# Split queries and keys stored once and repeated by the reads, on one core of Trainium2

## The reference, cut to what matters

```python
h = _layernorm(x, ln_w, ln_b)             # then a causal convolution over three tokens, giving h
q, k, v = jnp.split(h @ attn_w, 3, axis=-1)
q = q * cos + _rotate_half(q) * sin       # 16 heads of 8 dimensions
k = k * cos + _rotate_half(k) * sin
scores = jnp.einsum('bqhd,bkhd->bhqk', q, k) / jnp.sqrt(jnp.float32(D))
scores = jnp.where(causal, scores, jnp.float32(-1e+30))
p = jax.nn.softmax(scores, axis=-1)
y = jnp.einsum('bhqk,bkhd->bqhd', p, v).reshape(B, T, C)
```

## Time and profile before

| | us |
|---|---|
| median of 3 runs | 341.47 (338.66 to 347.56) |
| the profiled execution, its own time | 340.81 |
| its span in the trace | 338.6 |
| PE busy | 315.3 (93% of the span) |
| DVE busy | 245.2 (72%) |
| ACT busy | 220.0 (65%) |
| POOL busy | 128.1 (38%) |
| all 16 DMA engines, mean rate over the span | 66 GB/s |

### The profile page before, as it was taken

One profiled execution on the slowest core, in us unless ns is written; L12 is line 12 of the kernel. 1 busy time (PEld: TensorE's weight loads), 2 busy tenths in 40 slices (PEclk: granted clock), 3 DMA queues, 4 the chain that ended last, 5 costly groups with the idle time before them and its releaser, 6 DMA issues.

```text
span 338.6 us, 6802 instructions
## 1 busy us (share of the span) xinstructions
PE 315.3 (93%) x2270; PEld 220.6 (65%) x2270; DVE 245.2 (72%) x758; ACT 220.0 (65%) x649; POOL 128.1 (38%) x183
## 2 busy tenths in 40 slices
PE   8799989998989999999989998998999999999886
PEld 3348778665554433345446998985778687878675
DVE  4988875784898988888811552479788877887576
ACT  1488885375365756756676765754676667686995
POOL 3455564110641444410640440410685434535400
PEclk9999999999999999999998999999999999999999
DMA  7590000076763430091001003100100000000002
GB/s 213 196 274 10 2 0 2 8 243 170 209 206 89 113 102 3 1 326 52 5 31 56 2 31 111 33 1 2 54 20 15 0 2 1 3 0 0 2 0 65
DMA packets 21881, 22.47 MB, mean 66 GB/s; under 512 B 3894, under 2 KB 18646, under 8 KB 21846
## 3 DMA queue, kind: packets, MB, share of 16 engines
q1 hardware_dynamic: 18982, 16.78, 17.4%
q10 hardware_dynamic: 2352, 4.20, 3.7%
q0 software_dynamic: 512, 1.05, 1.0%
HBM read 14.22 MB, written 7.60 MB: 64 GB/s over the span
## 4 chain that ended last, share of the span: by engine, by line
PE 58%; DVE 16%; ACT 14%; issue 5%; POOL 4%; DMA 3%; SPq 0%; ACTq 0%; POOLq 0%
PE PS L1388 51%; PE PS L1442 5%; DVE PS L872 5%; ACT big L1167 5%; ACT big L1364 3%; POOL big L529 2%; DVE big L690 2%; DVE big L715 2%; DMA big<-in_A_WkT 2%; ACT big L1305 1%; ACT big L1141 1%; DMA XN<-scr_y,pos 1%; DVE XN L667 1%; ACT cw L1141 1%; PE PS L1704 1%
## 5 line engine op out<-in xcount | busy, mean ns | idle before, releaser
L1388 PE MATMUL PS<-big 128*128 128x128 f32 (+10 forms) x592 | 93.3, 308 | 7.0 <-DVE big L690 2.1
L1388 PEld LDWEIGHTS PS<-big 128*128 128x128 f32 (+3 forms) x592 | 56.2, 150 | 39.7 <-DVE mB L872 18.2
L529 POOL TENSOR_TENSOR big<-big,urec 128x1024 f32<-128x1024 f32 x24 | 45.6, 1900 | 60.2 <-DVE urec L722 45.4
L1167 ACT ACTIVATE big<-big 128x154 f32<-128x154 f32 x192 | 60.5, 319 | 10.6 <-DVE big L690 5.6
L872 DVE CUSTOM_DVE_ANT_0 PS<-PS,later 128x128 f32<-128x128 f32 (+3 forms) x128 | 60.1, 517 | 8.9 <-PE PS L1388 7.7
L1305 ACT ACTIVATE big<-PS 128x1024 f32<-128x1024 f32 (+3 forms) x64 | 43.2, 701 | 25.0 <-PE PS L1388 25.0
L1141 ACT ACTIVATE big<-PS 128x1280 f32<-128x1280 f32 (+2 forms) x30 | 32.3, 1088 | 27.0 <-PE PS L1442 24.5
L1388 PE MATMUL PS<-kkC,XT 128*128 128x462 f32 (+1 forms) x96 | 36.0, 511 | 1.9 <-DVE big L715 1.9
L1167 ACT ACTIVATION_READ_ACCUMULATOR big<-big 128x1 f32 x192 | 36.2, 189 | 0.0
L517 POOL TENSOR_TENSOR rstd<-ve,minus_half 128x4 f32<-128x4 f32 (+2 forms) x13 | 13.2, 1017 | 56.3 <-DVE ve L662 56.3
L1388 PEld LDWEIGHTS PS<-vwCm,big 128*128 128x128 f32 x256 | 30.8, 192 | 3.9 <-ACT big L1141 1.3
(11 more groups left out here) (192 smaller groups left out, 499.7 us busy)
## 6 DMA issues: line engine op xcount, KB each, us to landing
scr_qk<-big SPq DMA_DIRECT2D x12, 384.0 KB, 3.3
big<-scr_qk SPq DMA_DIRECT2D x16, 288.0 KB
big<-in_wv ACTq DMA_DIRECT2D x1, 2048.0 KB, 7.9
scr_x<-zrow SPq DMA_DIRECT2D x2, 448.0 KB, 6.9
scr_y<-big SPq DMA_DIRECT2D x2, 448.0 KB, 3.4
X<-in_x ACTq DMA_DIRECT2D x2, 256.0 KB, 3.3
big<-in_A_WoT ACTq DMA_DIRECT2D x1, 512.0 KB, 4.7
cw<-in_C_Wk SPq DMA_DIRECT2D x1, 512.0 KB, 5.2
```

The costliest lines, as they stand in the source:

```text
L529: pool.tensor_tensor(pn[:, 0:GH * P].rearrange("p (h k) -> p h k", h=GH), Pt[u % 3][:, :, 0:KM], r.to_broadcast([P, GH, KM]), ALU.mult).th ...
L1167: i = act.activation(Pt[u % 3][:, h, :], Pt[u % 3][:, h, :], ACT.Exp, accum_out=usum[:, u % 3, h:h + 1])
L1388: return pe.matmul(o, lhsT, rhs, start=start, stop=stop)
```

## The change

What it does, in six points:

1. `scr_qk` holds each part once (24 rows for keys, 24 for queries, per sequence). The six writes of a sequence are 128x512 of bf16 (128 KB) each instead of 384 KB.
2. The reads repeat rows. The keys of a group are still one DMA into 72 partitions, but its source has three outer steps of stride 0, then the 24 rows. The queries of a group are three DMAs, one for each x, into 24 partitions each; the source of each has three outer steps of stride 0, then 8 rows. `stack_ready` is awaited at 64 instead of 32.
3. On VectorE the second norm b is moved ahead of the split of sequence 0; `weigh_router` is moved from step 1 of the attention to before `rotate(1)`.
4. Folds: the second `queries_keys` stands at fold 25 instead of 30, the turn of norm b at 17 instead of 26, and the tasks m begin after fold 25 instead of 31. 24 folds lie between the tasks instead of 18; four tasks (`M_TWICE`) are followed by two folds.
5. For sequence 0 the constant columns of `vaug` are set by two memsets on POOL instead of two copies on ScalarE.
6. TensorE's wait ahead of the first task is for the copies of all but the last two folds; the whole of them is awaited at task 2. The first turn of maxima stands after fold 40.

```diff
         PS = ctx.enter_context(nc.psum_tensor("PS", [P, 8, 512], F32))
-        scr_qk = nc.dram_tensor("scr_qk", (B, 2, SPLIT, HB, T), BF16, kind="Internal").ap()
+        scr_qk = nc.dram_tensor("scr_qk", (B, 2, 3, SPLIT // 9, HB, T), BF16, kind="Internal").ap()
...
         F_UNIT = (3, 6, 9)
-        F_QKV = (14,30)
-        F_LN = 26
-        F_LATE = 32
-        F_VALUES = 42
-        F_MAX = 45
+        F_QKV = (14, 25)
+        F_LN = 17
+        F_LATE = 26
+        F_VALUES = 38
+        F_MAX = 41
+        M_TWICE = (5, 9, 13, 17)
...
             for b in range(B):
                 for a in range(3):
                     sp.wait_ge(part_ready[b], a + 1)
-                    sp.dma_start(scr_qk[b, 1].rearrange("(x y d) h t -> y (d h) x t", x=3, y=3)[a],
-                                 P3[:, 1, a, :].unsqueeze(1).to_broadcast([P, 3, T])).then_inc(scr_written[b], 16)
-                    sp.dma_start(scr_qk[b, 0].rearrange("(x y d) h t -> x (d h) y t", x=3, y=3)[a],
-                                 P3[:, 0, a, :].unsqueeze(1).to_broadcast([P, 3, T])).then_inc(scr_written[b], 16)
+                    for j in (1, 0):
+                        sp.dma_start(scr_qk[b, j, a].rearrange("d h t -> (d h) t"), P3[:, j, a, :]).then_inc(scr_written[b], 16)
                 if b:
                     store_maxima(0)
                 sp.wait_ge(scr_written[b], 16 * 6)
                 for g in range(HB // HG):
                     hs = slice(HG * g, HG * g + HG)
-                    sp.dma_start(ks[b][0:SPLIT, hs, :], scr_qk[b, 1, :, hs, :]).then_inc(stack_ready[b][g], 16)
-                    sp.dma_start(qs[b][0:SPLIT, hs, :], scr_qk[b, 0, :, hs, :]).then_inc(stack_ready[b][g], 16)
+                    parts = [scr_qk[b, j, :, :, hs, :].rearrange("a d h t -> a d (h t)") for j in range(2)]
+                    sp.dma_start(ks[b][0:SPLIT, hs, :].rearrange("r h t -> r (h t)"),
+                                 parts[1].unsqueeze(0).to_broadcast([3, 3, SPLIT // 9, HG * T])).then_inc(stack_ready[b][g], 16)
+                    for x in range(3):
+                        sp.dma_start(qs[b][SPLIT // 3 * x:SPLIT // 3 * (x + 1), hs, :].rearrange("r h t -> r (h t)"),
+                                     parts[0][x].unsqueeze(0).to_broadcast([3, SPLIT // 9, HG * T])).then_inc(stack_ready[b][g], 16)
...
             pool.wait_ge(part_ready[1], 3)
+            pool.wait_ge(preC_act, sum(j[2] for j in PREC[:F_VALUES]))
+            v = vaug[:, 0].rearrange("p t h m -> p (t h) m")
+            pool.memset(v[:, :, HDB:HDB + 1], 1.0).then_inc(v_ready, 1)
+            pool.memset(v[:, :, HDB + 1:32], 0.0).then_inc(v_ready, 1)
             split_maxima(1)
...
@@ -860,11 +875,12 @@
             add_tile("A", NT - 1)
             ln_u_stats(1)
             rotate(0)
+            ln_b_stats(1)
             add_rotated()
+            ln_apply("b", U, XN, 1)
             split_first()
-            ln_b_stats(1)
-            ln_apply("b", U, XN, 1)
             convolve(1)
+            weigh_router()
             rotate(1)
...
-                if s == 1:
-                    weigh_router()
-                elif s == 3:
+                if s == 3:
...
             def values(b):
                 v = vaug[:, b].rearrange("p t h m -> p (t h) m")
                 copy(v[:, :, 0:HDB], XN[:, QT * b:QT * b + QT, :].rearrange("p t (h d) -> p (t h) d", h=HB)).then_inc(v_ready, 1)
-                copy(v[:, :, HDB:HDB + 1], ones[:, 0:QT * HB].unsqueeze(2)).then_inc(v_ready, 1)
 
             def no_values(b):
                 v = vaug[:, b].rearrange("p t h m -> p (t h) m")
+                copy(v[:, :, HDB:HDB + 1], ones[:, 0:QT * HB].unsqueeze(2)).then_inc(v_ready, 1)
                 copy(v[:, :, HDB + 1:32], ones[:, 0:32 - HDB - 1].unsqueeze(1).to_broadcast([P, QT * HB, 32 - HDB - 1]),
                      0.0).then_inc(v_ready, 1)
...
-            copy_C(F_LN, F_VALUES)
+            copy_C(F_LN, F_MAX)
+            copy_maxima(0)
             act.wait_ge(preC_act, sum(j[2] for j in PREC[:F_VALUES]))
             values(0)
-            no_values(0)
-            copy_C(F_VALUES, F_MAX)
-            copy_maxima(0)
             copy_C(F_MAX, len(PREC))
...
@@ -1611,7 +1615,7 @@
             fold_C(F_LN, F_QKV[1])
             queries_keys(1)
             fold_C(F_QKV[1], F_LATE)
-            pe.wait_ge(preC_act, sum(j[2] for j in PREC[:F_LATE]))
+            pe.wait_ge(preC_act, sum(j[2] for j in PREC[:F_LATE - 2]))
...
                 if m % M_CHUNK == 0:
-                    pe.wait_ge(stack_ready[0][m // M_CHUNK], 32)
+                    pe.wait_ge(stack_ready[0][m // M_CHUNK], 64)
                 if m >= 3:
                     pe.wait_ge(s_max, m - 2)
+                elif m == 2:
+                    pe.wait_ge(preC_act, sum(j[2] for j in PREC[:F_LATE]))
                 for j in range(2):
                     i = scores_of(0, 2 * hp + j, qt, PS[:, first_bank(m) + j, 0:(qt + 1) * P])
                 i.then_inc(s_mm, 1)
...
             late = F_LATE
             for m in range(M0):
                 scores_for_maximum(m)
-                if m >= 2 and late < len(PREC):
+                for _ in range(2 if m in M_TWICE else 1):
                     fold_C(late, late + 1)
                     late += 1
-                if late == F_MAX:
-                    turn_maxima(0)
+                    if late == F_MAX:
+                        turn_maxima(0)
+            assert late == len(PREC)
```

More of the change, by code:

```diff
@@ L816, in ln_b_stats, with weigh_router @@
                 ln_stats("b", U, b, lambda: dve.wait_ge(ln_norm["u"], QT * b + QT))
+            def weigh_router():
+                dve.wait_ge(ld_b, 64)
+                dve.wait_ge(ld_vec, 16)
+                dve.wait_ge(zeroed, Z_ALL)
+                dve.tensor_scalar(rw2[:], rw[:], vec[:, V_LN2W:V_LN2W + 1], None, ALU.mult).then_inc(rw2_ready, 1)
+                dve.tensor_scalar(ln2b[:], ones[:], vec[:, V_LN2B:V_LN2B + 1], None, ALU.mult).then_inc(rw2_ready, 1)
             def convolve(b):
@@ L916, in x_plus_u @@
                 own.wait()
-            def weigh_router():
-                dve.wait_ge(ld_b, 64)
-                dve.wait_ge(ld_vec, 16)
-                dve.wait_ge(zeroed, Z_ALL)
-                dve.tensor_scalar(rw2[:], rw[:], vec[:, V_LN2W:V_LN2W + 1], None, ALU.mult).then_inc(rw2_ready, 1)
-                dve.tensor_scalar(ln2b[:], ones[:], vec[:, V_LN2B:V_LN2B + 1], None, ALU.mult).then_inc(rw2_ready, 1)
             def centre_router():
@@ L1654, in ring_scores @@
                 if n % M_CHUNK == 0:
-                    pe.wait_ge(stack_ready[b][n // M_CHUNK], 32)
+                    pe.wait_ge(stack_ready[b][n // M_CHUNK], 64)
                 if k < 2:
```

## The result

The changed kernel takes 367.5 us (median of 6 runs, 365.68 to 373.45) against 347.44 of the kernel before on the same chip (6 runs, 338.66 to 347.93). Some executions of any kernel fall into a slower state of the chip with a lower granted clock (four of these six of before, 347.3 to 347.9 us, and the changed kernel's 373.45), and all ratios here leave them out. The ratio is 1.079 [1.071, 1.087]: slower by 27 us. The profiled execution took 365.95 us, its span is 364.1.

What follows compares the result with a forecast made beforehand. TensorE, busy 41.48 of 44.42 us in the reordered stage, was taken as the bound, not DMA. Profiled 340.81 + 24.1 (step 8 late behind reads) + 1.5 (clock) = 366.4; median 0.66 higher, so 367; range 360 to 400.

Steps and rivals of the forecast that it cites:

- The term that decides: Reads of queries and keys: three engines carry them, 8.1 us per group instead of 2.8, making step 8 24.1 us late.
- VectorE and the order: Norm ahead of the split: split ends at 76.2, 3.8 us later; second queries and keys begin near 78.4 instead of 82.20.
- Writes: Sequence 0's writes at 128 KB: last issued at 76.6, landing 2.4 us later, first read issued at 79.0.
- Reads: Group reads on three engines at 23.9 GB/s each (bounds 16.5 and 26.1): 8.1 us per group, where it took 2.8.
- The step that decides: In the reads, a source's outermost step of three limits each DMA to three engines, a share of 0.18 to 0.20.
- Who waits: Attention steps behind SP's reads: step 0 at 115.8, step 4 at 125.5, step 8 at 150.0, the last 24.1 us late.
- All of SP's transfers pass through the same engines in order: SP's queue: small DMAs and writes wait behind reads, so the third small DMA lands at 150.0.
- landing over 15 us after its issue: Sign in the new profile: the third small DMA, behind SP's reads, lands over 15 us after its issue.
- The clock: TensorE's idle time ahead of step 8 brings one drop to 1.2 GHz for about 3 us, costing 1.5 us.
- The rest: Router weights, POOL constants, six more folds cost nothing; SP's 16 more reads at about 0.35 us hidden; median 0.66 above profiled.
- The rival on the other side: Reads spread as now, group 0 at 83.5, step 0 at 104.9, 1.9 us won, 339.5 us in all; chance 0.11.
- the DMA term: Step 8 waiting for its small DMA behind three-engine reads: 24.1 us added to the profiled 340.81.

Runs made afterwards that it cites:

- e2: The kernel before with only the changed transfers (queries and keys stored once, rows repeated by the reads): ratio 1.064 to the kernel before.
- e5: The changed kernel with a group's rows reordered so reads have outermost steps of 8 and 24 (8 engines, six reads per group): ratio 1.031 to before.
- e3: The kernel before with stored rows in three blocks of 24, one unused row between, nothing read twice: ratio 1.086 to before.
- e9: The changed kernel with rows laid so every read has an outermost step of 24 or 72 on both sides (12 engines): ratio 1.011 to before.
- e12: The kernel before with one edit, sequence 0's value constants written by POOL instead of ScalarE: ratio 0.995, median 338.8 us.
- e6: The kernel before with the single-storing transfers of e5 (8 engines) and POOL's constants: ratio 1.017 to before.
- e8: The kernel e5 with the second queries and keys put back behind four of five folds, and the wait for all copies restored: ratio 1.017 to before.
- e10: The kernel before with the single-storing transfers of e9 (12 engines) and POOL's constants: ratio 0.998 to before.
- e1: The changed kernel's whole order with the transfers of before (three stored copies, 72-row reads): ratio 1.018, median 345.4 us.
- e11: The changed kernel with norm first, four of five folds put back, all-copies wait restored, transfers on 12 engines: ratio 0.995, median 341.45 us.

## Why the prediction was right

The forecast was 367 with step 8 at 150.0; measured were 367.5 and 150.32. The term that decides was right, and several smaller ones were wrong and offset each other, which was luck. By its own steps:

- **VectorE and the order.** Nearly as worked out. The split ends at 76.9, not 76.2, because POOL's root outlasts the add. The timeline of DVE, against the earlier trace rows:

```profile
69.72 0.17 DVE L669 TENSOR_SCALAR ve<-mv 128x4 f32<-128x4 f32 x1
69.80 1.22 DVE L857 TENSOR_TENSOR big<-big 128x1024 f32<-128x1024 f32 x1
71.92 1.12 DVE L674 TENSOR_SCALAR XN<-U,mv,rstd 128x128 f32<-128x128 f32 x4 [0.90 <-POOL rstd L520]
...
75.66 1.22 DVE L868 TENSOR_TENSOR big<-big 128x1024 bf16<-128x1024 f32 x1
```

- **Writes.** Mis-sized. The last of six is issued at 77.3 (76.6 was predicted), lands 3.5 us later instead of 2.4, and the first read is issued at 80.81 (79.0). The six writes of sequence 0 (window 70:80), issue in ns, first and last start in us, and landing:

```profile
L473 SPq DMA_DIRECT2D scr_qk<-big x6: 319/380/433, 73.7 to 77.3; - x6
DMA to landing us min/median/max: 1.7/1.8/3.5
```

  The first five land in 1.7 to 2.0 us. With the same writes e2 and e5 issue the first read at 74.45 and 78.73, 1.8 us after the last write; why one landing takes 3.5 is open.

- **Reads.** The step that decides was right: 3 engines, share 0.19, shown by e3, e5 and e9 to come from the outermost steps and not from the repetition. The rate was 25.7 GB/s per engine, near the upper bound of 26.1; 7.6 us per group instead of 8.1. (The 8.1 is a slip: 48 pieces of 4,096 bytes at 23.9 GB/s are 8.2 us, so by its own terms step 8 was due at about 151, and the sum was 368.)
- **Who waits.** Right in its places: step 0 at 117.05 (115.8), step 4 at 127.48 (125.5), step 8 at 150.32 (150.0). At step 8 three errors cancel. The reads start 1.8 us late. Eight groups are 0.54 us quicker each, 4.3 in all. Between the first read and step 8 another 2.8 us pass that are neither (69.5 from 80.81 to 150.32, less 8 x 7.56, is 9.0 where the forecast had 71.0 less 8 x 8.1, or 6.2). The work ahead of step 0 ends at 114.95, so only 2.09 us there are a wait. "All of SP's transfers pass through the same engines in order" was right as far as it goes. What it lacked is that the list itself stops: the third set lay ready 5.4 us before SP issued it. The sign "landing over 15 us after its issue" holds from the first of the set (134.74 to 150.3), not for the last (12.6).
- **The clock.** The forecast added 1.5 us for one drop. From step 8 to the next start of its kind it took 12.28 us (162.60 less 150.32), where a stretch of full clock takes 9.40 (125.75 to 135.15 in e12, and the same in before): 2.9 us lost. Against that, before's own drop at 176 to 180 has no counterpart in the changed kernel (1.00 in every window of 4 us from 160 us on). From step 8 to the end of the span before took 212.7 us and the changed kernel 213.8, a net 1.1. Two errors that offset each other.
- **The rest.** "SP issues 16 more reads at about 0.35 us" was wrong by a factor of two. It took 0.68. It was hidden behind three engines, and it decided e5, e6 and e8. The median of the runs lies 1.5 us above the profiled execution, not 0.66.
- **The rival on the other side** was wrong as a mechanism. It gave 339.5 us, 1.9 won, for reads that are spread. e9 is that case and is 1.1% slower. The step that fails is "Then group 0 lands at 80.7 + 2.8 = 83.5, just when TensorE is ready." TensorE is ready then (87.82 less 4.30 of idle time), but the first read is issued at 80.20 and the first scores start at 87.82. Idle time of 4.3 us and some 4.5 us lost at 0.50, 0.50 and 0.88 from 88 to 100 are about what step 0 (113.25) misses the rival's 104.9 by. It took the six more folds as work that merely moves, and did not ask what TensorE does while it waits in their old place, nor what the clock does after that.

So the total was right because the DMA term, 22 of the 27 us, was right. The 6 us that the order costs by itself stood in the forecast only as a later start of the reads, which gives nearly the same number while the reads are the bound. That was luck, too: with quick reads the same working was off by 5.9 us (339.5 against 345.4).

## What to carry to other kernels

Before you repeat, block or pad a DMA's source, look at the slowest step that is not one, on both sides: its largest common divisor up to 16 is the number of engines, and a view that looks free can cost three quarters of them. Look as well at what shares the queue: count the issues ahead of each small urgent DMA, at the time they take with the new shapes. And when products are moved sooner, ask what covers the wait for the next thing in line; work taken from there is paid as idle time and then again at half clock.

## What the runs showed of the hardware that was not expected

- **Issue time depends on the shape.** A read of 72 plain rows takes SP 0.33 to 0.37 us; one of 24 rows with a repetition or a second step inside 0.64 to 0.70; e9's read of 24 x 3 rows 0.76 to 0.83, and its three plain ones of 24 rows 1.34 together (0.45). The changed kernel's plain write of 128 rows takes 0.32 to 0.43, before's with three copies 0.36 to 0.54 when nothing is behind. What sets this is open.
- **More engines, less each.** 3 engines do 25.7 GB/s each on these reads, 8 do 17 (138/(0.52 x 16)), 12 do 11 to 13 (140 in e10 at 0.78; 155 and 175 in e9 at 0.77 and 0.83), and before's unrepeated reads 16.5 on 12. So on 12 engines instead of 3 the rate was about twice as high, not four times. What holds them back, and whether the repetition is part of it, was not tried.
- **The clock after idle time.** Ahead of the first scores: idle 8.18 us, then 0.50 until about 96; 5.16 (e1), 0.50 until 96 and 0.79 for the next 4; 4.30 (e9), 0.50 until 96 and 0.88 for the next 4; 3.38 (e5) and 2.11 (e11), 0.57 in 88 to 92 alone; 2.92 (e8), no drop there; 0.52 (before, e10, e12), none either. At step 8, 0.32, 0.59 and 0.79 us of idle time (e10, e9, e11) brought no drop, 2.34 (e8) one to 0.50 from 128 to 136 us, 3.04 (e5) one of over 8 us. So the length of the gap alone does not tell: 2.11 us were followed by a drop and 2.92 were not, and e12 shows 0.65 at 108 to 112 behind a gap of 0.60.
